# Attention inside a decoder layer: summing the softmax probabilities by GpSimd and accumulating DMAs in place of GpSimd groups, and loops that hint their back edge

## Chip, cores and metric

One core of a Trainium2 chip runs the whole layer in one launch. The metric is device time in microseconds (us); the kernel before takes 5611.14 us, the median of 3 runs (5606.75 to 5614.59).

## What is computed

The layer is self-attention, cross-attention and a gated feed-forward with weights rounded to FP4, each with a residual. Only the self-attention is changed. Its core, per batch element and head (2 x 16 heads of 32 channels, 2048 positions), is run twice, once with a bias that decays with distance and once without:

```python
scores = einsum('bhqd,bhkd->bhqk', q, k) / sqrt(hd)
if bias is not None:
    scores = scores + bias[None, None]
attn = softmax(scores, axis=-1)
out = einsum('bhqk,bhkd->bhqd', attn, v)
...
out = alpha * out_short + (1.0 - alpha) * out_long
```

The softmax needs, per query, the sum of the exponentials over all 2048 keys. The change is about how that sum, the denominator, is formed.

## The kernel before, in words

`project` computes q, k and v in four groups and rounds the feed-forward weights, `attend` does the attention, `finish` the rest. In `attend` a **unit** is one head with one of the two biases: 64 units in all, four to a pass, 16 passes (`UNITS`, `PASSES`). The first and the last pass are written out, and the 14 between them are a loop on each engine (`Fori`), so each engine comes to a back edge 13 times. A unit is 16 **steps** (`KB`), one for each block of 128 keys.

In a step TensorE (PE in the profile) does four things, in an order written out by hand in its `one_pass`:

- `times_v` (L903): four fp32 products of the block's exponentials with v, shown as eight matmuls, into the bank `outputs_T`;
- `scores_for_exp` (L836, tile scores_kq): four pieces of 512 queries of the next blocks' transposed scores, which ScalarE (ACT) exponentiates into `probs_T` (L745), a ring of `PBUF` = 8 blocks of 128 x 2048 fp32;
- `scores_for_max` (L836, tile scores_qk): four pieces of the scores of a later unit, which VectorE (DVE) reduces to row maxima (L764);
- in some steps `count` (L913): the matmuls of a summed group with a matrix of ones, which adds the column sums into the bank `sums`.

The denominator goes by six **groups** of key blocks (`GROUPS`: four of three blocks, two of two). GpSimd (POOL) adds the blocks of a group in SBUF (L704, ten additions of 128 x 2048 a unit) into one of two buffers `group_sum`, and three steps later (`COUNT_LAG`) TensorE counts the group. So there are six counts a unit. After the last one, ScalarE copies the sums out of PSUM (`take_sums`, L724, at its step 4 of the next unit), VectorE inverts them in four pieces (L786, steps 3 to 6, `INVERT`), scales the output (L792, step 8, `WEIGH`) and for every second unit adds the two heads' parts (L799, step 10, `MIX`).

What holds the engines together: GpSimd's queue runs in order, and each addition waits for ScalarE's exponentials of its block and, at the start of a group, for the count that frees the buffer. ScalarE may write block b + 8 only when `times_v` and the addition of block b are done. SyncE's queue loads q, k and v of the unit four further on (L619, L621, L625) when the unit's last transposed scores are done. Nothing in the kernel before is issued as a DMA from GpSimd's queue, and none of its DMAs accumulates.

Of the kernel before, what the change touches and what calls it, by code (L numbers as in the profile page):

```python
# [16 lines left out]
F32 = mybir.dt.float32  # L17
# [190 lines left out]
def project(nc, x, w, weights, xg, x_in, qk_scr, v_scr, w_gate, w_up, w_down, wgu, wd_scr):  # L208
# [4 lines left out]
    with ExitStack() as ctx:  # L213
# [63 lines left out]
        def over_groups(eng, group):  # L277


            with eng.Fori(0, B * NG // 2 - 1) as m:  # L280
# [235 lines left out]
INVERT = 3  # L516
WEIGH = 8
MIX = 10


GROUPS = ((0, 1, 2), (3, 4, 5), (6, 7, 8), (9, 10, 11), (12, 13), (14, 15))
COUNT_LAG = 3
GROUPS_N = len(GROUPS)
ADDS = KB - GROUPS_N


def adds_until(kb):

    return sum(max(0, sum(b <= max(kb, g[1]) for b in g) - 1) for g in GROUPS if g[0] <= kb)

# [11 lines left out]
def attend(nc, qk_scr, v_scr, gates, kinkA, kinkB, pos_scr, attn_scr):  # L542
# [4 lines left out]
    with ExitStack() as ctx:  # L547
# [10 lines left out]
        group_sum = sb("probs_group_sum", [P, 2, L], F32)  # L558
# [32 lines left out]
        counted = Rises(sem("a_counted"), UNITS * GROUPS_N, credit=1)  # L591
# [16 lines left out]
        def _(sp):  # L608
# [64 lines left out]
            with sp.Fori(1, PASSES - 1) as n:  # L673
                one_pass(n, False, False)
# [6 lines left out]
        def _(pool):  # L681
            give_credit(pool, [maxed, expd, summed, added, counted, taken, sums_out, weighed] + stored)
# [7 lines left out]

            def one_pass(n):
                for w in range(UNITS):
                    for g, blocks in enumerate(GROUPS):

                        wait_apart(pool, counted, counted.at(n, w * GROUPS_N + g - 1), passed)
                        total = group_sum[:, g % 2, :]
                        for b in blocks[1:]:

                            wait_apart(pool, expd, expd.at(n, (w * KB + b + 1) * NQ), passed)
                            first = probs[:, blocks[0] % PBUF, :]  # L700
                            if b > blocks[1]:
                                first = total
                                wait_apart(pool, added, added.at(n, w * ADDS + adds_until(b) - 1), passed)
                            nc.gpsimd.tensor_tensor(total, first, probs[:, b % PBUF, :], ALU.add).then_inc(added.sem, 1)  # L704

            with pool.Fori(0, PASSES) as n:
# [3 lines left out]
        def _(act):  # L710
# [10 lines left out]
            def take_sums(w, n):  # L721
                act.wait_ge(counted.sem, counted.at(n, (w + 1) * GROUPS_N))
# [5 lines left out]
            def one_pass(n, first, last):  # L728
                for w in range(UNITS):
                    back = unit_before(w, n, first)  # L730
                    for kb in range(KB):

                        if back and kb == COUNT_LAG + 1:
# [15 lines left out]
            with act.Fori(1, PASSES - 1) as n:  # L749
# [5 lines left out]
        def _(dve):  # L755
# [65 lines left out]
            with dve.Fori(1, PASSES - 1) as n:  # L821
# [9 lines left out]
        def _(pe):  # L831
# [16 lines left out]
            def scores_for_max(w, n, c):  # L848
# [6 lines left out]
                pe.wait_ge(maxed.sem, maxed.at(n, k - 2 + (k - 3) // CHUNKS if k >= 3 else 0))  # L855
# [51 lines left out]
            def count(w, n, g):  # L907

                if g == 0:
                    pe.wait_ge(sums_out.sem, sums_out.at(n, w))  # L910
                pe.wait_ge(added.sem, added.at(n, w * ADDS + adds_until(GROUPS[g][-1])))
                for qt in range(NQ):
                    last = nc.tensor.matmul(pc[qt * HD:(qt + 1) * HD, :], ones[:, :], group_sum[:, g % 2, qt * BANK:(qt + 1) * BANK],  # L913
                                            start=g == 0, stop=g == GROUPS_N - 1)
                last.then_inc(counted.sem, 1)
# [10 lines left out]
            def one_pass(n, first, last):  # L926
                for w in range(UNITS):
# [8 lines left out]
                    for i in range(KB):  # L936
# [8 lines left out]
                        due = [(u, g) for g in range(len(GROUPS)) for u, d in (((w, n), 0), (back, KB))  # L945
# [446 lines left out]
```

## Time and profile before

| | |
|---|---|
| median of 3 runs | 5611.14 us (5606.75 to 5614.59) |
| span of the profiled execution | 5613.5 us (the profile gives no other time for it) |
| TensorE busy | 5382.8 us, 96% of the span |
| VectorE busy | 4180.9 us, 74% |
| ScalarE busy | 2874.8 us, 51% |
| GpSimd busy | 2933.2 us, 52% |
| attention | about 690 to 4280 us of the span |
| mean granted TensorE clock | 0.981 of 2.4 GHz |

Matmuls are pipelined and their recorded ends are modelled, so a TensorE that is busy all the time isn't at its peak. What a stretch costs is read from the distance between the starts of its instructions. "<-issue" means that the engine waited for nothing the profile shows. A DMA's "us to landing" runs from its issue until its semaphore rises.

### The profile page before, as it was taken

The numbers are of one execution on the slowest core, as the hardware profiler recorded it, in microseconds if no ns is written. First come the engines' busy times: TensorE is split into PE (matmuls) and PEld (weight loads), VectorE is DVE, ScalarE is ACT, GpSimd is POOL, SyncE is SP. The second block draws the span as 40 slices with busy tenths as digits, with TensorE's granted clock in tenths as the row PEclk, the third lists the DMA queues.
The fourth block names the chain that finished last, engine by engine and source line by source line (L and its number), as shares of the span: only waits on it lengthen the run. The fifth ranks groups of instructions, "written<-read, shape, count | busy, mean of one in ns | idle before, by whom it ended". The sixth has DMA issues, their size and how long they took to land. (4 is left out here: it accounts for less than half of the span.)

```text
span 5613.5 us, 97704 instructions
## 1 busy us (share of the span) xinstructions
PE 5382.8 (96%) x28780; PEld 2121.9 (38%) x28780; DVE 4180.9 (74%) x7218; ACT 2874.8 (51%) x5201; POOL 2933.2 (52%) x658
## 2 busy tenths in 40 slices
PE   7999899999999999999999999999996999999999
PEld 3444333333322323223233332232332555555555
DVE  5444688877877878778778787787883777777777
ACT  1111166666666666666666666666664333333332
POOL 0000088878877878778778787788884000000000
PEclk9999799999999999999999999999998999999999
DMA  4333201010101010101010101010101000000000
GB/s 135 105 104 93 81 19 33 21 29 22 33 21 29 21 34 21 29 21 33 22 29 21 34 21 29 21 33 22 29 3 49 17 22 17 22 17 22 17 22 12
DMA packets 145632, 191.62 MB, mean 34 GB/s; under 512 B 18500, under 2 KB 97988, under 8 KB 145030
## 3 DMA queue, kind: packets, MB, share of 16 engines
q1 hardware_dynamic: 145159, 185.65, 11.2%
q8 instruction: 255, 4.18, 0.3%
q14 instruction: 218, 1.79, 0.1%
HBM read 123.56 MB, written 61.64 MB: 33 GB/s over the span
## 5 line engine op out<-in xcount | busy, mean ns | idle before, releaser
L764 DVE TENSOR_REDUCE rowmax_parts<-scores_qk 128x1 f32<-128x512 f32 x4096 | 2569.8, 682 | 668.9 <-PE scores_qk L836 666.3
L745 ACT ACTIVATE probs_T<-scores_kq 128x512 f32<-128x512 f32 x4096 | 2263.3, 596 | 1249.5 <-PE scores_kq L836 1195.2
L704 POOL TENSOR_TENSOR probs_group_sum<-probs_T 128x2048 f32<-128x2048 f32 x384 | 1742.4, 4538 | 667.4 <-PE sums L913 395.7
L836 PE MATMUL scores_kq<-q_operand,k_operand 103*128 103x512 f16 (+3 forms) x3712 | 1279.8, 351 | 16.7 <-ACT probs_T L745 15.4
L704 POOL TENSOR_TENSOR probs_group_sum<-probs_group_sum,probs_T 128x2048 f32<-128x2048 f32 x256 | 1185.5, 4631 | 46.0 <-POOL probs_group_sum L704 45.1
L836 PE MATMUL scores_qk<-k_operand,q_operand 96*128 96x512 f16 (+4 forms) x3712 | 1178.9, 354 | 22.8 <-DMA k_operand<-positions_dram 18.5
L903 PE MATMUL outputs_T<-probs_T,v_operand 128*32 128x512 f32 x8192 | 1103.3, 611 | 52.4 <-issue 52.4
L836 PEld LDWEIGHTS scores_qk<-k_operand,q_operand 96*128 96x128 f16 (+1 forms) x3712 | 352.7, 98 | 898.6 <-DVE rowmax_parts L764 627.1
L1341 PE MATMUL f_gate_up<-w_gate_up,xq_T 128*128 128x352 f32 x2048 | 626.4, 462 | 0.8 <-issue 0.8
L836 PEld LDWEIGHTS scores_kq<-q_operand,k_operand 103*128 103x128 f16 x3712 | 361.2, 98 | 672.9 <-ACT probs_T L745 507.1
L1341 PEld LDWEIGHTS f_gate_up<-w_gate_up,xq_T 128*128 128x128 f32 x2048 | 382.5, 190 | 200.7 <-issue 2.6
L913 PE MATMUL sums<-probs_group_sum,ones 128*32 128x512 f32 x3072 | 417.6, 616 | 3.3 <-POOL probs_group_sum L704 3.3
L836 PE MATMUL scores_kq<-q_operand_above,k_operand 103*128 103x512 f16 (+3 forms) x1152 | 398.8, 347 | 0.8 <-ACT probs_T L745 0.6
L836 PE MATMUL scores_qk<-k_operand,q_operand_above 102*128 102x512 f16 (+3 forms) x1152 | 388.0, 352 | 3.8
L473 PE MATMUL products_p<-xn_T,w_qkv 128*128 128x512 f32 x768 | 337.7, 595 | 0.8 <-ACT xn_T L418 0.8
L1330 PE MATMUL f_gate_up<-w_down,hidden_T 128*128 128x512 f32 x704 | 330.8, 597 | 3.4 <-DVE hidden L1249 2.7
L683 POOL MEMSET ones<- 128x32 f32 x1 | 0.1, 124 | 602.5 <-POOLq L213 602.5
L903 PEld LDWEIGHTS outputs_T<-probs_T,v_operand 128*32 128x32 f32 x8192 | 161.8, 108 | 372.2 <-issue 352.0
L786 DVE RECIPROCAL sums_inverse<-sums_T 128x128 f32<-128x128 f32 x256 | 240.7, 942 | 15.5 <-ACT sums_T L724 15.5
L494 PE MATMUL products_p<-w_qkv,xn_T 128*128 128x512 f32 x512 | 221.1, 592 | 0.0
L473 PEld LDWEIGHTS products_p<-xn_T,w_qkv 128*128 128x128 f32 x768 | 144.4, 191 | 172.2 <-issue 172.2
L1128 ACT ACT_TABLE_LOAD x160 | 205.3, 1283 | 2.8
(144 smaller groups left out, 3477.2 us busy)
## 6 DMA issues: line engine op xcount, KB each, us to landing
qk_parts_dram<-qk_parts SPq DMA_DIRECT2D x96, 256.0 KB, 2.5
q_operand<-qk_parts_dram SPq DMA_DIRECT2D x192, 128.0 KB, 2.6
k_operand<-qk_parts_dram SPq DMA_DIRECT2D x192, 128.0 KB, 2.9
v_dram<-v_heads SPq DMA_DIRECT2D x16, 1024.0 KB, 5.4
v_operand<-v_dram SPq DMA_DIRECT2D x64, 256.0 KB, 3.1
q_operand_above<-qk_parts_dram SPq DMA_DIRECT2D x96, 128.0 KB, 2.8
x_groups<-x SPq DMA_DIRECT2D x8, 1024.0 KB, 8.8
attention_dram<-o_mixed SPq DMA_DIRECT2D x128, 64.0 KB, 1.6
```

Source lines behind the costliest of these rows:

```text
L473: last = nc.tensor.matmul(mm[:, m % 4, :], w[:, c, m * P:(m + 1) * P], xT[:, u, c, :], start=c == 0, stop=c == KT - 1)
L494: last = nc.tensor.matmul(mm[:, j % 4, :], xT[:, u, c, t * P:(t + 1) * P], w[:, c, (3 + a) * H:(4 + a) * H], start=c == 0, stop=c == KT - 1)
L704: nc.gpsimd.tensor_tensor(total, first, probs[:, b % PBUF, :], ALU.add).then_inc(added.sem, 1)
L745: nc.scalar.activation(probs[:, kb % PBUF, qt * BANK:(qt + 1) * BANK], pb[:, k % 2, :], ACT.Exp)\
L764: nc.vector.reduce_max(rowmax[:, w % 2, c // NQ, c % NQ:c % NQ + 1], pa[:, k % 3, :], AX.X)\
L786: nc.vector.reciprocal(inv[:, r * P:(r + 1) * P], sums[:, r * P:(r + 1) * P]).then_inc(inverted.sem, 1)
L836: return nc.tensor.matmul(out, lhsT, rhs, start=start, stop=stop, skip_group_check=True)
L903: last = nc.tensor.matmul(po[qt * HD:(qt + 1) * HD, :], v_op[:, w, kb, :], probs[:, kb % PBUF, qt * BANK:(qt + 1) * BANK], start=kb == 0, ...
L913: last = nc.tensor.matmul(pc[qt * HD:(qt + 1) * HD, :], ones[:, :], group_sum[:, g % 2, qt * BANK:(qt + 1) * BANK], start=g == 0, stop=g = ...
L1128: nc.scalar.activation(warmed[:, place:place + 1], eps[:, 0:1], function)
L1330: last = nc.tensor.matmul(pg[:, 0, 0, :], hT[:, c, :], wd[:, c, :], start=c == 0, stop=c == FT - 1)
L1341: last = nc.tensor.matmul(pg[:, k % 2, g, 0:FW], xqT[:, t, c, :], wgu[:, c, g, k * FW:(k + 1) * FW], start=c == 0, stop=c == KT - 1)
```

## The change

- GpSimd now adds nine blocks (0, 1, 3, 5, ... 15) by eight additions into one of two `added_sum` buffers. The other seven (2, 4, ... 14) go by DMAs issued from GpSimd's queue into one buffer, `poured_sum`: the first is a plain copy of 1 MB within SBUF, and the six that follow accumulate. Each waits in GpSimd's queue until the one before it has landed. The first also waits until TensorE has counted the buffer's last content.
- TensorE counts twice a unit: the poured sum in step 3 of the next unit, the added sum in step 4. The order of scores and maxima, which differed in steps with a count, is the same in all steps now.
- ScalarE waits, before it overwrites a block of the ring, for the addition or for the DMA that reads it. It takes the sums at its step 6. VectorE inverts them in steps 6 to 9, weighs at 11 and mixes at 12.
- The waits of TensorE for VectorE at the first three pieces of a pass are written by the piece that used the bank last.
- All loops (in `project`, `attend`, `finish`) carry `hint_back_edge=True`.

The core of the diff:

```diff
-GROUPS = ((0, 1, 2), (3, 4, 5), (6, 7, 8), (9, 10, 11), (12, 13), (14, 15))
-COUNT_LAG = 3
+INVERT = 6
+WEIGH = 11
+MIX = 12
+SUMMED_BY_POOL = (0, 1, 3, 5, 7, 9, 11, 13, 15)
+SUMMED_BY_DMA = (2, 4, 6, 8, 10, 12, 14)
+COUNT_POURED, COUNT_ADDED = 3, 4
+TAKE_SUMS = 6
...
+            def add(w, n, b):
+                total = added_sum[:, w % 2, :]
+                if b == 1:
+                    first = probs[:, 0, :]
+                    wait_apart(pool, counted, counted.at(n, w - 1), passed)
+                else:
+                    first = total
+                    wait_apart(pool, added, added.at(n, w * ADDS + adds_until(b) - 1), passed)
+                wait_apart(pool, expd, expd.at(n, (w * KB + b + 1) * NQ), passed)
+                nc.gpsimd.tensor_tensor(total, first, probs[:, b % PBUF, :], ALU.add).then_inc(added.sem, 1)
+
+            def pour(w, n, b):
+                i = SUMMED_BY_DMA.index(b)
+                wait_apart(pool, expd, expd.at(n, (w * KB + b + 1) * NQ), passed)
+                if i == 0:
+                    wait_apart(pool, counted_poured, counted_poured.at(n, w), passed)
+                    nc.gpsimd.dma_start(poured_sum[:, :], probs[:, b % PBUF, :]).then_inc(poured.sem, 16)
+                else:
+                    wait_apart(pool, poured, poured.at(n, w * POURS + i), passed)
+                    nc.gpsimd.dma_start(poured_sum[:, :], probs[:, b % PBUF, :], accum_op=ALU.add).then_inc(poured.sem, 16)
+
+                    for b in range(1, KB):
+                        if b in SUMMED_BY_DMA:
+                            pour(w, n, b)
+                        else:
+                            add(w, n, b)
...
-                        old = w * KB + kb - PBUF
-                        act.wait_ge(summed.sem, summed.at(n, old + 1))
-                        act.wait_ge(added.sem, added.at(n, old // KB * ADDS + adds_until(old % KB)))
+                        u, b = divmod(w * KB + kb - PBUF, KB)
+                        act.wait_ge(summed.sem, summed.at(n, u * KB + b + 1))
+                        if b not in SUMMED_BY_DMA:
+                            act.wait_ge(added.sem, added.at(n, u * ADDS + adds_until(b)))
+                        elif u >= 0 or not first:
+                            act.wait_ge(poured.sem, poured.at(n, u * POURS + SUMMED_BY_DMA.index(b) + 1))
...
                         times_v(w, n, i)
-                        if due:
-                            maxima(0)
-                            scores(i + 1, 2)
-                            maxima(1)
-                            scores(i + 1, 3)
-                        else:
-                            scores(i + 1, 2)
-                            maxima(0)
-                            scores(i + 1, 3)
-                            maxima(1)
-                        for u, g in due:
-                            count(*u, g)
+                        if back and i == COUNT_POURED:
+                            count_poured(*back)
+                        if back and i == COUNT_ADDED:
+                            count_added(*back)
+                        scores(i + 1, 2)
+                        maxima(0)
+                        scores(i + 1, 3)
+                        maxima(1)
...
-            with pe.Fori(1, PASSES - 1) as n:
+            with nc.Fori(1, PASSES - 1, engines=[pe.engine], hint_back_edge=True) as n:
```

## Rows read from the trace of the kernel before

**Rows 1.** The page: busy time, share of the span and instructions by engine.

```profile
PE 5382.8 (96%) x28780; PEld 2121.9 (38%) x28780; DVE 4180.9 (74%) x7218; ACT 2874.8 (51%) x5201; POOL 2933.2 (52%) x658
```

**Rows 2.** The waits in the attention, 692.9 to 4267.4 us: total, times, longest.

```profile
ACT probs_T L745 <- PE scores_kq L836: 1194.0, 1388, 6.9
...
POOL probs_group_sum L704 <- PE sums L913: 395.7, 126, 10.7
...
PE outputs_T L903 <- issue: 52.4, 13, 4.6
```

**Rows 3.** The timeline of TensorE: plain steps, and the first one with a count.

```profile
2000.13 1.06 PE L903 MATMUL outputs_T<-probs_T,v_operand 128*32 128x512 f32 x8
...
2003.06 1.06 PE L903 MATMUL outputs_T<-probs_T,v_operand 128*32 128x512 f32 x8
...
2004.72 0.38 PE L836 MATMUL scores_kq<-q_operand,k_operand 103*128 103x512 f16 x1
2005.03 1.07 PE L913 MATMUL sums<-probs_group_sum,ones 128*32 128x512 f32 x8
2006.03 0.39 PE L836 MATMUL scores_qk<-k_operand,q_operand 102*128 102x512 f16 x1
2006.25 0.38 PE L836 MATMUL scores_kq<-q_operand,k_operand 103*128 103x512 f16 x1
...
2007.06 1.06 PE L903 MATMUL outputs_T<-probs_T,v_operand 128*32 128x512 f32 x8
```

**Rows 4.** The timeline of TensorE: first product of successive units in one pass.

```profile
2035.04 1.93 PE L903 MATMUL outputs_T<-probs_T,v_operand 128*32 128x512 f32 x8 [3.97 <-issue]
...
2093.08 1.06 PE L903 MATMUL outputs_T<-probs_T,v_operand 128*32 128x512 f32 x8
...
2146.99 1.06 PE L903 MATMUL outputs_T<-probs_T,v_operand 128*32 128x512 f32 x8
...
2201.90 1.06 PE L903 MATMUL outputs_T<-probs_T,v_operand 128*32 128x512 f32 x8
...
2260.51 1.93 PE L903 MATMUL outputs_T<-probs_T,v_operand 128*32 128x512 f32 x8 [3.58 <-issue]
```

**Rows 5.** Stretches at a back edge: length, busy of five engines, granted clock, DMA share, GB/s.

```profile
2031.07:2034.90 3.83, 0.00 (x0) 0.00 (x0) 1.04 (x2) 0.68 (x2) 0.00 (x0) 0.95 0.05 10
2035.00:2041.00 6.00, 5.68 (x20) 0.80 (x20) 1.38 (x2) 1.20 (x2) 0.00 (x0) 0.50 0.02 5
2041.00:2047.00 6.00, 6.00 (x43) 2.03 (x39) 4.15 (x7) 3.41 (x7) 5.35 (x2) 0.97 0.00 0
```

**Rows 6.** The timeline: TensorE's first and last unit, and what ends the attention.

```profile
692.86 1.93 PE L903 MATMUL outputs_T<-probs_T,v_operand 128*32 128x512 f32 x8
...
4223.13 1.06 PE L903 MATMUL outputs_T<-probs_T,v_operand 128*32 128x512 f32 x8
...
4273.35 0.59 ACT L724 COPY sums_T<-sums 128x512 f32<-128x512 f32 x1 [6.43 <-PE sums L913]
```

**Rows 7.** The timeline of VectorE: reciprocals between the maxima.

```profile
2053.31 0.94 DVE L786 RECIPROCAL sums_inverse<-sums_T 128x128 f32<-128x128 f32 x1
2054.17 2.42 DVE L764 TENSOR_REDUCE rowmax_parts<-scores_qk 128x1 f32<-128x512 f32 x4
2056.50 0.94 DVE L786 RECIPROCAL sums_inverse<-sums_T 128x128 f32<-128x128 f32 x1
```

**Rows 8.** The timeline of GpSimd: two additions behind each other.

```profile
2041.48 4.54 POOL L704 TENSOR_TENSOR probs_group_sum<-probs_T 128x2048 f32<-128x2048 f32 x1 [10.61 <-PE sums L913]
2046.20 4.54 POOL L704 TENSOR_TENSOR probs_group_sum<-probs_group_sum,probs_T 128x2048 f32<-128x2048 f32 x1 [0.18 <-POOL probs_group_sum L704]
```

**Rows 9.** DMA issues by tile: KB each, median us from issue to landing.

```profile
v_dram<-v_heads SPq DMA_DIRECT2D x16, 1024.0 KB, 5.4
...
x_groups<-x SPq DMA_DIRECT2D x8, 1024.0 KB, 8.8
...
attention_dram<-o_mixed SPq DMA_DIRECT2D x128, 64.0 KB, 1.6
```

**Rows 10.** Stretches (share and GB/s last): all DMA engines busy, loads, attention; SyncE's issues.

```profile
4290.00:4300.00 10.00, 6.56 (x16) 3.15 (x16) 2.03 (x6) 2.93 (x5) 0.00 (x0) 0.62 1.00 378
...
2024.00:2034.00 10.00, 6.16 (x41) 2.01 (x39) 5.90 (x10) 4.33 (x8) 4.80 (x2) 1.00 0.38 111
...
692.90:4267.40 3574.50, 3497.72 (x22439) 1092.63 (x22442) 2840.61 (x4490) 2298.76 (x4216) 2923.01 (x639) 0.99 0.09 25
...
2025.02 1.26 SPq L619 DMA_DIRECT2D q_operand<-qk_parts_dram  x3
```

**Rows 11.** The chain that ended last, in `finish`: successive tiles, start and length.

```profile
4374.10 4.87 PE f_gate_up L1341 x16
...
4414.45 4.79 PE f_gate_up L1341 x16
...
4454.64 4.87 PE f_gate_up L1341 x16
...
4494.90 4.77 PE f_gate_up L1341 x16
```

**Rows 12.** VectorE's groups over two passes, 2035.0 to 2485.8 us.

```profile
L792 DVE SCALAR_TENSOR_TENSOR o_weighed<-o_T,gates,sums_inverse 128x512 f32<-128x512 f32 x8 | 6.2, 773 | 0.0
...
L799 DVE TENSOR_TENSOR o_mixed<-o_weighed 128x512 f32<-128x512 f32 x4 | 2.7, 684 | 0.0
```

More of the change, by code:

```diff
@@ L277, in over_groups @@
         def over_groups(eng, group):
-            with eng.Fori(0, B * NG // 2 - 1) as m:
+            with nc.Fori(0, B * NG // 2 - 1, engines=[eng.engine], hint_back_edge=True) as m:
                 for u in range(2):
@@ L672, in _ @@
             one_pass(0, True, False)
-            with sp.Fori(1, PASSES - 1) as n:
+            with nc.Fori(1, PASSES - 1, engines=[sp.engine], hint_back_edge=True) as n:
                 one_pass(n, False, False)
@@ L706, in _ @@
-            with pool.Fori(0, PASSES) as n:
+                    for b in range(1, KB):
[3 more added lines that the diff above has]
+                            add(w, n, b)
+            with nc.Fori(0, PASSES, engines=[pool.engine], hint_back_edge=True) as n:
                 one_pass(n)
@@ L748, in _ @@
             one_pass(0, True, False)
-            with act.Fori(1, PASSES - 1) as n:
+            with nc.Fori(1, PASSES - 1, engines=[act.engine], hint_back_edge=True) as n:
                 one_pass(n, False, False)
@@ L820, in _ @@
             one_pass(0, True, False)
-            with dve.Fori(1, PASSES - 1) as n:
+            with nc.Fori(1, PASSES - 1, engines=[dve.engine], hint_back_edge=True) as n:
                 one_pass(n, False, False)
@@ L853, in scores_for_max @@
                     pe.wait_ge(opened[w].sem, opened[w].at(n, opened[w].per_pass))
-                pe.wait_ge(maxed.sem, maxed.at(n, k - 2 + (k - 3) // CHUNKS if k >= 3 else 0))
+                if k >= 3:
+                    pe.wait_ge(maxed.sem, maxed.at(n, k - 2 + (k - 3) // CHUNKS))
+                else:
+                    m = max(j for j in range(UNITS * CHUNKS) if j % 3 == k)
+                    pe.wait_ge(maxed.sem, maxed.before(n, m + 1 + m // CHUNKS))
                 bank = pa[:, k % 3, :]
@@ L971, in _ @@
             end = (UNITS - 1, PASSES - 1)
-            for g in range(GROUPS_N):
-                if GROUPS[g][-1] + COUNT_LAG >= KB:
-                    count(*end, g)
+            count_poured(*end)
+            count_added(*end)
 CTX, CD = 77, 1024
@@ L1067, in over_tiles @@
             step(-1, 1, (1, 2))
-            with eng.Fori(0, NT // 2 - 1) as m:
+            with nc.Fori(0, NT // 2 - 1, engines=[eng.engine], hint_back_edge=True) as m:
                 for t in range(2):
@@ L1094, in _ @@
             sp.dma_start(wd[:, :, :], wd_scr[:, :, :]).then_inc(wd_in, 16)
-            with sp.Fori(0, NT // 2 - 1) as m:
+            with nc.Fori(0, NT // 2 - 1, engines=[sp.engine], hint_back_edge=True) as m:
                 for t in range(2):
```

52 lines of the change are left out of this document (22 added, 30 removed).

## The prediction

> **What bounds the kernel now.** I read the page first. TensorE is busy for 96% of the span, and the change lies in the attention, where VectorE and GpSimd follow at 74% and 52% over all [rows 1]. The waits of that stretch come next: ScalarE waits 1194 us for TensorE's scores, GpSimd 396 us for counts, while TensorE's own matmuls wait only in 13 places, 52.4 us, for nothing the profile shows [rows 2]. So TensorE sets the pace. Its timeline gives the price of its work by the distance of starts: a plain step takes 2.93 us and the step with a count 4.00 [rows 3]. Within that one, the count moves the next score from the usual 0.22 us behind the last to 1.31, so a count costs 1.09 us.
>
> The starts of four successive units [rows 4] are 58.04, 53.91, 54.91 and 58.61 us apart. The two in the middle are plain, with a mean of 54.41; the others hold a back edge. A whole pass is 225.47 us, which is 7.8 more than four plain units. Where it goes is seen in the windows: TensorE does nothing for some 3.9 us, then works for 6 us at a granted clock of 0.50 (1.2 GHz) before it is back at 0.97 [rows 5]. The stall thus costs about 4 us itself and nearly as much again by the clock that follows it. There are 13 of them: 13 x 7.8 = 101 us. As a check, 63 x 54.41 + 101 = 3529, against 3530.3 from the first unit to the last [rows 6].
>
> **The change, part by part.** The sum is made against the profiled execution, span 5613.5 us, which is 2.4 us above the median.
>
> *Counts.* Four of six go: 4 x 1.09 = 4.4 us a unit. All of it is on TensorE, so a unit would fall from 54.4 to 50.0.
>
> *The other engines' schedule.* A step with a reciprocal keeps VectorE busy for 3.19 us (distance of two reciprocals) [rows 7] against TensorE's 2.93 to 3.05. Before, one of the four such steps had a count of TensorE beside it, worth a microsecond of slack. Now steps 6 to 9 have none, at 0.15 to 0.25 us each: +0.8 a unit. The weighing and mixing move between steps of the same kind, ScalarE's copy of the sums likewise; I cost these, the reordering and the waits at a pass's first pieces at nothing, since ScalarE waits for TensorE anyway [rows 2]. If that cover went, each would cost at most its own 0.6 to 0.8 us. TensorE and VectorE together would allow a unit of **50.8 us**.
>
> *GpSimd's queue.* It becomes add, pour, add, pour. An addition takes 4.72 us from start to start [rows 8]. A pour holds the queue while it is issued, and the next one holds it until the last has landed, with the additions behind it. No row shows an issue by GpSimd. SyncE's takes 0.42 us (three in 1.26) [rows 10]; I take 1.0, an estimate, with 0.4 and 2 as bounds.
>
> No row shows an accumulating DMA either. One pass over 1 MB with all 16 engines busy ran at 378 GB/s [rows 10], so 1,048,576 bytes take 2.77 us. What a small DMA needs beside its bytes is about 1.4 us (64 KB landed in 1.6) [rows 9]. If the second read (of the old sum) is hidden behind the first, a pour lands in 1.4 + 2.8 = 4.2 us. If it is not, in 1.4 + 5.5 = 6.9. If it also runs at the rate of the store of 1 MB (5.4 us, so 4.0 beside the 1.4), in 1.4 + 8.0 = 9.4. I take 6.9, since a pour must fetch two operands for each it writes, and its rows of 8 KB are long like those of the 378 GB/s stretch and not short like the store's.
> The Trainium skill (Collectives: The Full Stack, The bandwidth ceiling) says the same of reductions in general: two reads for each write, half of a copy's rate. No run here shows it yet. Its page DMA: Bandwidth & Descriptors (Anatomy of one DMA) gives about 2.0 us plus bytes over 436 GB/s for a DMA issued from GpSimd. With two reads that is 6.8 us, with one 4.4, and the sum below would be 51.6 or, with the queue no longer deciding, 50.8.
>
> The unit on GpSimd's queue: the first pour is plain and lands behind the addition, 1.0 + 4.72 = 5.7. Five more go by the landing, 5 x 6.9 = 34.5. The seventh is followed by two additions (15, then 1 of the next unit), which cover it: 1.0 + 2 x 4.72 = 10.4. That is 50.6. SyncE's loads of the later unit are on the same 16 DMA engines and fall on pour 12: a share of 0.38 over 10 us is 3.8 us of all engines [rows 10]. Half of it is taken: +1.9, bounds 0 and 3.8. So the queue needs **52.5 us** a unit, and it, not TensorE, sets the pace by 1.7 us. TensorE's count of the poured sum then waits for the last pour, and ScalarE's ring of eight blocks takes up the lag until then.
>
> *Back edges.* With the stall and the half clock gone, the 101 us go. The queue must not hide them: 52.5 a unit holds for every unit. In `finish` tiles are 40.35, 40.19 and 40.26 us apart, with or without a back edge [rows 11], so at most 0.1 us for each of 14: nothing. `project` has two back edges and no wait for them.
>
> *The end.* The last unit had 50.2 us from its first product to the copy of its sums [rows 6]. Now its seven pours follow each other from about 10.7 us on: 10.7 + 5.7 + 5 x 6.9 + 6.9 = 57.8, and two counts make it 60: +10.
>
> **Sum:** 63 x 52.5 = 3307.5 for 3530.3, which is -222.8, +10: -213. From 5613.5 that is 5400.5, and against the median **5398 us**.
>
> **Rivals.**
> - *The pours keep up.* If most of the second read is hidden or the loads don't collide, TensorE and VectorE set 50.8 us: 63 x 50.8 = 3200, -330 and nothing at the end: **5281**. For it: the DMA engines' share in the attention is only 0.09 [rows 10]. Against it: two operands pass through each engine for each result. Chance 0.20.
> - *Slower: the chain of pours is the bound.* Each microsecond of landing costs five a unit. The queue needs 18.0 + 5 x landing, so it passes the mean unit of before (3530.3 / 63 = 56.0) at a landing of 7.6 us, only 0.7 above my value. At 9.4 a unit is 65.0: 63 x 9.0 = +567, and the end's +25: **6203**. TensorE would then idle several microseconds a unit, and it has been seen what a stall of 4 us does to its clock [rows 5]. For it: a plain DMA of 1 MB already took 5.4 us as a store and 8.8 as x's load, in shorter rows and beside others [rows 9]. Against it: long rows ran at 378 GB/s. Chance 0.21.
> - *VectorE holds GpSimd off.* The weighing and half a mixing a unit, 0.77 + 0.34 = 1.1 us [rows 12], read two operands from SBUF. If GpSimd's issues have to wait for all of that, a unit takes 53.6: 63 x 1.1 = +69, **5467**. For it speaks only that both touch SBUF; against it, additions follow each other by 4.72 us beside VectorE's work [rows 8]. Chance 0.04.
>   [...]
> - *The hint does nothing.* TensorE's stall (7.8 a pass) is then mostly taken up by the queue's margin (4 x 1.7), but GpSimd's own fetch would stand in its chain: 13 x 4 = 52 us more, **5450**. Against it: the stalls come once a pass, at the back edge and nowhere else [rows 2, 4]. Chance 0.08.
> - *It comes out even*, the landing at 7.6: 0.03.
>
> **How the numbers follow.** The forecast's own case (landing 6.4 to 7.4, 5300 to 5560) has 0.44. The range must take in the 5281 and leave out the upper part of the slow case: 5260 to 5690, which is a landing up to 7.8 us. Some 0.16 lie above and 0.03 below. A measurement of this kernel tells about 0.2% (11 us) from no change. Faster: 0.44 + 0.20 + 0.04 + 0.08 = 0.76; same 0.03; slower 0.21.
>
> **What would show it.** The median landing of `poured_sum` 6.4 to 7.4 us, the DMA share in the attention near (2.8 + 6 x 5.5) / 52.5 + 0.09 = 0.77. GpSimd idle before every other pour, not for ScalarE but for its own DMA. Two counts a unit, steps of 3.0 us without one, about 3.2 in steps 6 to 9. No wait "<-issue" of 4 us and no stretch at clock 0.50 every pass. It is wrong if the landing is over 7.6 (then GpSimd's wait grows in every pair and ScalarE waits for `poured_sum`), or if TensorE waits nowhere in a unit (then the pours keep up).

## The result: 195 us slower, and the profile after

The changed kernel takes **5806.65 us** (median of 4 runs, 5802.63 to 5819.8) against 5611.6 us of the kernel before on the same chip: a ratio of 1.0352, 95% interval 1.0338 to 1.0367. The forecast was 5398 us with a range of 5260 to 5690, so it had both the sign and the range wrong.

The page of the kernel after, its lines on engines, clock, DMA share, the two DMA queues and the groups that matter (line 706 is an addition, 717 an accumulating pour, 938 a count, 931 the product with v):

```profile
span 5800.3 us, 95123 instructions
...
PE 5238.4 (90%) x26732; PEld 2122.1 (37%) x26732; DVE 4268.2 (74%) x7218; ACT 2901.8 (50%) x5201; POOL 2707.7 (47%) x978
...
PEclk9999799999999999999999999999998999999999
DMA  4332376666666666667666676666665000000000
...
q0 software_dynamic: 64512, 469.79, 37.9%
q1 hardware_dynamic: 145159, 185.65, 10.8%
...
L717 POOL DMA_DIRECT2D probs_poured<-probs_T x384 | 338.9, 883 | 932.3 <-DMA probs_poured<-probs_T 697.8
...
L938 PE MATMUL sums<-probs_poured,ones 128*32 128x512 f32 x512 | 87.6, 762 | 132.5 <-DMA probs_poured<-probs_T 132.4
...
probs_poured<-probs_T POOLq DMA_DIRECT2D x448, 1024.0 KB, 7.2
```

TensorE is busy for 144 us less than before [rows 1], in a span that is 187 us longer. So it no longer sets the pace throughout: 90% against 96%. The mean granted clock fell from 0.981 to 0.956 of 2.4 GHz. The counts did go (4 x 1.09 us in 63 units are 275 us), and more than that came back, as idle time and as matmuls at half clock.

The waits in the attention show where (700 to 4400 us; total, times, longest), to be held against [rows 2]:

```profile
ACT probs_T L769 <- PE scores_kq L860: 1341.9, 1322, 9.4
...
POOL probs_poured L717 <- DMA probs_poured<-probs_T: 689.3, 231, 5.8
...
PEld sums L938 <- DMA probs_poured<-probs_T: 136.5, 43, 5.2
PE sums L938 <- DMA probs_poured<-probs_T: 116.0, 47, 4.7
...
PE scores_qk L860 <- DVE rowmax_parts L788: 128.2, 112, 3.9
...
POOL probs_poured L714 <- PE sums L938: 109.7, 43, 6.3
...
PE outputs_T L931 <- issue: 86.9, 13, 7.5
...
PE scores_kq L860 <- DMA q_operand_above<-negmax_T: 28.2, 25, 2.5
```

Before, TensorE's matmuls had one large wait, the 13 at back edges (and 15.2 us in 25 short waits for ScalarE, which the forecast passed over). Now there are four: for the last pour at the count (47 times), for VectorE's maxima (112 times), for SyncE's load of a unit's negated row maxima, `negmax_T`, in its step 14 (25 times), and still the 13 at the back edges, with 86.9 us in place of 52.4.

**What a unit costs, step by step.** From first product to first product a step's length can be read, and its mean taken over the 13 passes from the second to the 14th. The table sets the kernel after beside an experiment described below, plain_psum. There TensorE has no wait for a pour in a pass and none for `negmax_T`, and its waits for the maxima are down to 28.2 us (us; four units of a pass):

| unit | step 3, after / there | steps 11 to 14, after / there | step 15, after / there | unit, after / there |
|---|---|---|---|---|
| 0 | 4.25 / 3.91 | 19.04 / 13.07 | 3.02 / 3.02 | 60.36 / 54.00 |
| 1 | 7.48 / 3.79 | 14.43 / 11.89 | 3.41 / 3.02 | 56.66 / 50.03 |
| 2 | 6.59 / 3.91 | 16.02 / 13.10 | 3.02 / 3.02 | 57.29 / 51.65 |
| 3 | 8.24 / 3.79 | 12.98 / 11.90 | 9.77 / 7.88 | 62.42 / 54.89 |

Over all 63 distances the mean unit is 58.66 us against 56.04 before: 63 x 2.62 = +165 us. The end adds 16, and about 5 lie outside the attention, which makes the 187. Against plain_psum's 52.30, the differences of the columns sum to 11.2, 12.5 and 2.3 us a pass. Scaled to 63 units that is **176 us at the count of the pours, 197 us in steps 11 to 14, where the weighing and mixing lie**, and 36 us in step 15. Not all of the 197 us is VectorE's. In units 1 and 3, which have no mixing, step 14 alone is longer by 2.5 us a pass, 40 us over all. There TensorE waits for the load of `negmax_T`. That is a DMA of 4 KB, which landed in 1.7 us before and in 5.5 us in the kernel after (medians), and psum_operands (experiment 4), which has no delay on VectorE, still waits 24.9 us for it. So these 40 us are put down to the pours' traffic; no run isolates them.

**The first place, GpSimd's queue** (timeline; start, length, then in brackets the idle time before and what ended it). The forecast had these gaps at 6.9 us:

```profile
2001.30 0.88 POOL L717 DMA_DIRECT2D probs_poured<-probs_T  x1 [3.70 <-ACT probs_T L769]
2001.91 4.84 POOL L706 TENSOR_TENSOR probs_added<-probs_added,probs_T 128x2048 f32<-128x2048 f32 x1
2008.83 0.88 POOL L717 DMA_DIRECT2D probs_poured<-probs_T  x1 [2.08 <-DMA probs_poured<-probs_T]
2009.44 4.84 POOL L706 TENSOR_TENSOR probs_added<-probs_added,probs_T 128x2048 f32<-128x2048 f32 x1
2016.38 0.88 POOL L717 DMA_DIRECT2D probs_poured<-probs_T  x1 [2.09 <-DMA probs_poured<-probs_T]
...
2023.93 0.88 POOL L717 DMA_DIRECT2D probs_poured<-probs_T  x1 [2.11 <-DMA probs_poured<-probs_T]
...
2033.13 0.88 POOL L717 DMA_DIRECT2D probs_poured<-probs_T  x1 [3.76 <-DMA probs_poured<-probs_T]
2033.74 4.83 POOL L706 TENSOR_TENSOR probs_added<-probs_added,probs_T 128x2048 f32<-128x2048 f32 x1
2038.23 4.79 POOL L706 TENSOR_TENSOR probs_added<-probs_T 128x2048 f32<-128x2048 f32 x1
2046.38 0.59 POOL L714 DMA_DIRECT2D probs_poured<-probs_T  x1 [3.35 <-PE sums L938]
```

Successive pours start 7.53, 7.55, 7.55 and 9.20 us apart: each time the landing of the last one ends the wait. The addition lies inside the gap and is no bound (a pour's row is 0.88 us long, but the addition starts 0.61 behind it). From a landing to the start of the pour that waited for it pass 0.57 us, nearly always. The last line shows the chain start anew: the first pour of a unit waits until TensorE has counted the buffer.

TensorE at that count, in its timeline and in windows (columns as in [rows 5]; the last window is the whole attention):

```profile
2038.41 1.06 PE L931 MATMUL outputs_T<-probs_T,v_operand 128*32 128x512 f32 x8
...
2043.81 1.94 PE L938 MATMUL sums<-probs_poured,ones 128*32 128x512 f32 x8 [4.33 <-DMA probs_poured<-probs_T]
```

```profile
2038.41:2043.80 5.39, 1.06 (x9) 0.15 (x8) 1.19 (x2) 0.73 (x2) 4.62 (x2) 0.90 0.58 141
2043.80:2049.00 5.20, 5.19 (x18) 1.45 (x18) 1.99 (x4) 1.63 (x3) 2.60 (x2) 0.50 0.30 112
2049.00:2055.00 6.00, 6.00 (x39) 1.85 (x39) 3.35 (x6) 3.72 (x8) 5.44 (x3) 0.96 0.63 167
692.90:4400.00 3707.10, 3322.20 (x20245) 1086.26 (x20245) 2921.14 (x4486) 2300.12 (x4169) 2662.90 (x946) 0.95 0.67 149
```

It idles 4.33 us for the pour and then works 5.2 us at a granted clock of 0.50, as after a back edge before. A late pour is paid nearly twice, and since the next chain starts behind that count, GpSimd's queue gets the delay as well.

**The second place, VectorE** (timeline of one stretch, GpSimd, VectorE and TensorE together; 816 weighs, 823 mixes, 788 is a row maximum):

```profile
2129.82 4.84 POOL L706 TENSOR_TENSOR probs_added<-probs_added,probs_T 128x2048 f32<-128x2048 f32 x1
...
2131.92 3.30 DVE L816 SCALAR_TENSOR_TENSOR o_weighed<-o_T,gates,sums_inverse 128x512 f32<-128x512 f32 x1
...
2135.88 0.39 PE L860 MATMUL scores_qk<-k_operand,q_operand 96*128 96x512 f16 x1 [2.48 <-DVE rowmax_parts L788]
...
2138.85 4.84 POOL L706 TENSOR_TENSOR probs_added<-probs_added,probs_T 128x2048 f32<-128x2048 f32 x1
...
2140.52 3.73 DVE L823 TENSOR_TENSOR o_mixed<-o_weighed 128x512 f32<-128x512 f32 x1
```

A weighing that took 0.77 us [rows 12] takes 3.30: it begins 2.1 us into an addition of GpSimd and ends at 2135.22, 0.56 us after the addition's end (2134.66). TensorE's next score then waits for the maximum that was queued behind it. The tiles' own lines (least, median, longest in ns) show it for all of them; before they were 739/774/4552 and 680/682/692:

```profile
L816 DVE SCALAR_TENSOR_TENSOR o_weighed<-o_T,gates,sums_inverse x64: 742/1640/4678, 786.0 to 4459.5; 128x512 f32<-128x512 f32 x64
L823 DVE TENSOR_TENSOR o_mixed<-o_weighed x32: 682/2540/4556, 848.5 to 4460.3; 128x512 f32<-128x512 f32 x32
```

The Trainium skill (SBUF — State Buffer, SBUF: two separate sides) states just this: a VectorE operation with two SBUF inputs and a GpSimd operation that reads SBUF hold one pair of ports exclusively, whichever starts first, and the other is blocked until it ends. The trace agrees: the weighing above ends 0.56 us after the addition that it ran into.

### The profile page after: what moved, and what is told of

Same layout as the page of the kernel before. It is cut to its first block and busy times, and to the rows that moved or that the text cites. A ratio compares the mean times of both kernels' runs of the same rounds, so it can differ in the third digit from the quotient of the medians.

```text
span 5800.3 us, 95123 instructions
## 1 busy us (share of the span) xinstructions
PE 5238.4 (90%) x26732; PEld 2122.1 (37%) x26732; DVE 4268.2 (74%) x7218; ACT 2901.8 (50%) x5201; POOL 2707.7 (47%) x978
## 3 DMA queue, kind: packets, MB, share of 16 engines
q0 software_dynamic: 64512, 469.79, 37.9%
## 5 line engine op out<-in xcount | busy, mean ns | idle before, releaser
L788 DVE TENSOR_REDUCE rowmax_parts<-scores_qk 128x1 f32<-128x512 f32 x4096 | 2534.3, 679 | 750.0 <-PE scores_qk L860 749.6
L769 ACT ACTIVATE probs_T<-scores_kq 128x512 f32<-128x512 f32 x4096 | 2298.4, 597 | 1418.4 <-PE scores_kq L860 1357.3
L706 POOL TENSOR_TENSOR probs_added<-probs_added,probs_T 128x2048 f32<-128x2048 f32 x448 | 2145.9, 4790 | 9.8 <-ACT probs_T L769 9.0
L860 PE MATMUL scores_kq<-q_operand,k_operand 103*128 103x512 f16 (+3 forms) x3712 | 1310.0, 358 | 42.2 <-DMA q_operand_above<-negmax_T 28.6
L860 PE MATMUL scores_qk<-k_operand,q_operand 96*128 96x512 f16 (+4 forms) x3712 | 1150.3, 360 | 108.4 <-DVE rowmax_parts L788 77.9
L931 PE MATMUL outputs_T<-probs_T,v_operand 128*32 128x512 f32 x8192 | 1127.6, 623 | 87.8 <-issue 86.9
L717 POOL DMA_DIRECT2D probs_poured<-probs_T x384 | 338.9, 883 | 932.3 <-DMA probs_poured<-probs_T 697.8
L706 POOL TENSOR_TENSOR probs_added<-probs_T 128x2048 f32<-128x2048 f32 x64 | 308.0, 4812 | 64.9 <-ACT probs_T L769 64.9
L860 PEld LDWEIGHTS scores_kq<-q_operand_above,k_operand 103*128 103x128 f16 x1152 | 113.0, 98 | 350.4 <-ACT probs_T L769 293.8
L938 PE MATMUL sums<-probs_poured,ones 128*32 128x512 f32 x512 | 87.6, 762 | 132.5 <-DMA probs_poured<-probs_T 132.4
```

The costliest lines, as they stand in the source:

```text
L717: nc.gpsimd.dma_start(poured_sum[:, :], probs[:, b % PBUF, :], accum_op=ALU.add).then_inc(poured.sem, 16)
L769: nc.scalar.activation(probs[:, kb % PBUF, qt * BANK:(qt + 1) * BANK], pb[:, k % 2, :], ACT.Exp)\
L788: nc.vector.reduce_max(rowmax[:, w % 2, c // NQ, c % NQ:c % NQ + 1], pa[:, k % 3, :], AX.X)\
L860: return nc.tensor.matmul(out, lhsT, rhs, start=start, stop=stop, skip_group_check=True)
L931: last = nc.tensor.matmul(po[qt * HD:(qt + 1) * HD, :], v_op[:, w, kb, :], probs[:, kb % PBUF, qt * BANK:(qt + 1) * BANK], start=kb == 0, ...
L938: mm = nc.tensor.matmul(pc[qt * HD:(qt + 1) * HD, :], ones[:, :], src[:, qt * BANK:(qt + 1) * BANK], start=first, stop=last)
```

## The experiments

Each ran beside the kernel before on its own chip, where that one took 5612 to 5613 us. Each quotation is the text on record before the run.

**1 and 2. The hint alone, in both kernels.** hints_only is the kernel before with the hint on all loops, no_hints the kernel after without it.

```diff
-            with pe.Fori(1, PASSES - 1) as n:
+            with nc.Fori(1, PASSES - 1, engines=[pe.engine], hint_back_edge=True) as n:
```

> The kernel before with nothing changed but the hint on every loop's back edge. If the hint removes the fetch and the half clock behind it, the 13 stalls of 4 us and the clock go: about 5510 us. If the hint does nothing for a body of this size, the 13 stalls stay at 3.6 to 4.6 us and the time stays at 5611 within 10 us. The changed kernel's 13 stalls (6.7 us each) speak for the second.

> The changed kernel without the hints. If the hint does nothing: 5807 us within 12. If it does save part of the fetch, slower by up to 50 us, and the 13 stalls longer than 6.7 us.

hints_only: 5574.23 us, ratio 0.9929 (0.9912 to 0.9945). no_hints: 5857.77, ratio 1.0432 (1.0415 to 1.045). The hint is worth 38 us in the kernel before and 51 in the kernel after, neither the whole 101 nor nothing, so neither branch of the first expectation came true. The trace of hints_only shows what is left at a back edge (TensorE's waits, one of its products, and the window behind it):

```profile
PE outputs_T L903 <- issue: 16.5, 9, 2.2
```

```profile
1128.78 1.75 PE L903 MATMUL outputs_T<-probs_T,v_operand 128*32 128x512 f32 x8 [1.72 <-issue]
```

```profile
1129.00:1135.00 6.00, 5.87 (x32) 1.19 (x28) 2.42 (x4) 1.89 (x4) 1.01 (x1) 0.72 0.02 5
```

The stall falls from 4.0 us to about 1.8, and a lower clock still follows it, now a mean of 0.72 over 6 us. In the kernel after the stall is longer: 86.9 us / 13 = 6.7 with the hint, and 101.8 / 13 = 7.8 without.

**3. Pours that don't accumulate.** plain_pours copies each poured block over the last one, so that six of the seven are missing from the denominator; ScalarE's copy adds 1.0 so that it isn't zero.

```diff
-                    nc.gpsimd.dma_start(poured_sum[:, :], probs[:, b % PBUF, :], accum_op=ALU.add).then_inc(poured.sem, 16)
+                    nc.gpsimd.dma_start(poured_sum[:, :], probs[:, b % PBUF, :]).then_inc(poured.sem, 16)
```

> The changed kernel with the six accumulating DMAs of a unit turned into plain copies of the same 1 MB. Left out: six of seven poured blocks from the denominators (a constant 1 is added to the sums so that none is zero). Theory 1, the chain of pours is the bound: landing falls from 7.2 to about 4.4 us, the chain to some 45 us a unit, TensorE no longer waits for it, and the time falls to about 5500 to 5600. Theory 2, TensorE's own stalls (blocked VectorE, back edges, half clock) are the bound: it stays above 5700.

5789.46 us, ratio 1.0315 (1.0297 to 1.0332). The landing fell from 7.2 to 4.6 us, the pours' share of the DMA engines from 37.9% to 21.2%, and TensorE's wait at the count went: step 3 is 3.8 to 3.9 us in every unit. Yet only 17 us were gained. The page's line and those of the two tiles tell why:

```profile
probs_poured<-probs_T POOLq DMA_DIRECT2D x448, 1024.0 KB, 4.6
```

```profile
L816 DVE SCALAR_TENSOR_TENSOR o_weighed<-o_T,gates,sums_inverse x64: 751/3718/3973, 777.7 to 4445.0; 128x512 f32<-128x512 f32 x64
L823 DVE TENSOR_TENSOR o_mixed<-o_weighed x32: 681/3685/4887, 843.4 to 4445.8; 128x512 f32<-128x512 f32 x32
```

With the pours out of the way, weighing and mixing start early in an addition nearly every time: the median is 3.7 us each. Steps 11 to 14 are 6.5 us a unit longer than in plain_psum (26.0 a pass), where they were 3.1 in the kernel after. No matmul waits for `negmax_T` here. What one place gave up, the other took. It came out as the second expectation (above 5700) had it.

**4. Weighing and mixing with one operand in PSUM.** psum_operands writes the inverse sums, and the odd unit's weighed output, into a PSUM bank that is free then, and mixes right behind the weighing. All is computed. It puts a few waits of VectorE and TensorE for that bank in.

```diff
-                nc.vector.reciprocal(inv[:, r * P:(r + 1) * P], sums[:, r * P:(r + 1) * P]).then_inc(inverted.sem, 1)
+                nc.vector.reciprocal(pt[:, r * P:(r + 1) * P], sums[:, r * P:(r + 1) * P]).then_inc(inverted.sem, 1)
...
-                nc.vector.tensor_tensor(o_mix[:, p, :], o_w[:, 0, :], o_w[:, 1, :], ALU.add).then_inc(mixed.sem, 1)
+                nc.vector.tensor_tensor(o_mix[:, p, :], o_w[:, 0, :], pt[:, :], ALU.add).then_inc(mixed.sem, 1)
```

> The changed kernel with the inverse sums, and the second weighed output, kept in PSUM (bank turned), so that VectorE's weighing and mixing have one SBUF operand each, the mixing follows the weighing in step 11, and TensorE's transpose waits for both. If two SBUF operands make VectorE wait for GpSimd's addition, the weighing falls from a mean of 1.96 to about 0.8 us and the mixing from 2.65 to 0.8. If TensorE's side set the pace everywhere that would be 2.2 us a unit, 140 in all. If the chain of pours is the bound in most units, under 60 us come back, most of it in the units that follow a back edge.

5831.52 us, ratio 1.0388 (1.0371 to 1.0405): 25 us slower than the kernel after, where the expectation had up to 140 us or under 60 us come back, though the cause of delay on VectorE is gone. The weighing (now with `turned` in PSUM) is short every time; TensorE's wait for the pours has doubled:

```profile
L816 DVE SCALAR_TENSOR_TENSOR o_weighed<-o_T,gates,turned x32: 734/736/747, 781.5 to 4438.5; 128x512 f32<-128x512 f32 x32
```

```profile
PEld sums L938 <- DMA probs_poured<-probs_T: 276.1, 43, 9.6
PE sums L938 <- DMA probs_poured<-probs_T: 252.7, 47, 8.7
```

The time moved to step 3: 13.84, 8.85 and 11.72 us in units 1, 2 and 3. So with the lock gone the chain of pours alone makes the kernel as slow as the changed one, and (experiment 3) the lock alone does too.

**5. Both at once.** plain_psum is 3 and 4 together. If two bounds of nearly equal height stand behind each other, only this one falls far.

> Both edits at once: plain copies in place of the accumulating DMAs, and VectorE's second operand in PSUM. Left out, as before: six of seven poured blocks from the denominators (1 is added to the sums). Apart they gave 5789 and 5832 us. Theory A, two bounds of nearly the same height (the chain of pours by its landing, VectorE held by GpSimd's additions), each of which stays when only the other is taken away: together they leave TensorE's own 50.7 us a unit and some 2 for the back edge, so 5440 us, within 40. Theory B, something else sets 58.7 us a unit (GpSimd's additions, the half clock, the reordered steps): it stays above 5700.

**5391.49 us**, ratio 0.9609 (0.9593 to 0.9625). It is 49 us below the 5440 of theory A, 9 more than its margin. Alone the two edits gave -17 and +25 us, together -415. That settles the cause: two bounds, each of which alone holds the unit near 58.7 us (58.69 in experiment 3, 59.00 in experiment 4), and below them 52.30. Its units without a back edge are 50.04 and 51.65 us, mean 50.85; the forecast for TensorE and VectorE together was 50.8.

**6. Two buffers for the pours.** two_psum is 4 with `poured_sum` doubled, a semaphore for each, and counts, copy and inversions one step later. The chain no longer waits for TensorE's count.

```diff
-        poured_sum = sb("probs_poured", [P, L], F32)
+        poured_sum = sb("probs_poured", [P, 2, L], F32)
...
-                    wait_apart(pool, counted_poured, counted_poured.at(n, w), passed)
+                    wait_apart(pool, counted_poured, counted_poured.at(n, w - 1), passed)
```

> Accumulating pours as in the changed kernel, but into two buffers that alternate by unit (with a semaphore each), so that the first pour of a unit doesn't wait for TensorE's count; counts a step later, VectorE's operand in PSUM. If the coupling of the chain's start to TensorE's step 3 is what costs, the unit falls to TensorE's 53: 5450 us. If the chain's own length does (gaps of 5.2 + 42.0 + 9.6 in the changed kernel's trace), it stays at 56 to 57 a unit: 5700 us, within 50.

5751.68 us, ratio 1.0241 (1.0224 to 1.0258): 80 us less than experiment 4, but still slower than before, at the upper end of the second branch (5700, within 50). The 80 us are what the second buffer and the later count give together; how much of it is the coupling of TensorE's and the queue's delays, no run separates. What is left is the chain's own length: the mean unit is 57.95 us (56 to 57 expected), and GpSimd still waits 902 us for its own DMAs.

**7 and 9. Five pours in place of seven**, GpSimd adding eleven blocks, with the operands in PSUM (five_psum) and in SBUF as they were (five_only). The diff is what both have; five_psum has the edit of experiment 4 besides.

```diff
-SUMMED_BY_POOL = (0, 1, 3, 5, 7, 9, 11, 13, 15)
-SUMMED_BY_DMA = (2, 4, 6, 8, 10, 12, 14)
+SUMMED_BY_POOL = (0, 1, 2, 4, 5, 7, 8, 10, 11, 13, 14)
+SUMMED_BY_DMA = (3, 6, 9, 12, 15)
```

> Five blocks (3, 6, 9, 12, 15) poured, eleven added by ten additions, two additions between any two pours, VectorE's operand in PSUM. All is computed. The landing of 7.2 us lies behind two additions of 4.75, so nothing waits for it; GpSimd's queue needs 10 x 4.75 + 5 x 0.6 = 50.5 us a unit, TensorE about 52.8. Theory A gives 5440 us, within 50. If GpSimd's additions are slowed further by DMAs, or TensorE waits for the last pour, 5500 to 5600.

> The changed kernel with five blocks poured and eleven added, and nothing else: VectorE's weighing and mixing read two SBUF operands again. All is computed. Beside the run with five pours and the operand in PSUM (5491 us) it prices VectorE's wait for GpSimd's additions where the chain of pours is no bound. If that wait is as in the plain copies (some 6.4 us a unit between the two runs with and without it), about 5750 to 5850 us. If it was only a partner of the chain, 5491 to 5560.

five_psum: **5490.73 us**, ratio 0.9782 (0.9765 to 0.9798), with all computed and pours that land in 7.6 us. A pour is now due every third step, 8.8 us or more, and keeps up: no pour waits for the one before it. The time lies 51 us above the 5440 expected, for TensorE still waits 34.8 us for last pours, and the back edges cost more (below). five_only: 5670.73, ratio 1.0097 (1.0079 to 1.0116). That is between its two branches: the wait costs 2.9 us a unit here, not 6.4. The 180 us between the two runs are the edit of experiment 4, which moves the operand to PSUM and the mixing from step 12 to step 11. What moving the mixing alone would give was not run. The mixing shows it most plainly: in step 12 it starts some 0.4 us into an addition (2098.65 against 2098.28 in one case) and waits it out, 5 us in the median.

```profile
L816 DVE SCALAR_TENSOR_TENSOR o_weighed<-o_T,gates,sums_inverse x64: 750/1639/2855, 782.5 to 4326.8; 128x512 f32<-128x512 f32 x64
L823 DVE TENSOR_TENSOR o_mixed<-o_weighed x32: 691/4965/5004, 840.5 to 4327.6; 128x512 f32<-128x512 f32 x32
```

In five_psum each back edge costs more, for TensorE stalls twice (its timeline behind one of them):

```profile
1112.28 1.93 PE L931 MATMUL outputs_T<-probs_T,v_operand 128*32 128x512 f32 x8 [4.18 <-issue]
...
1118.60 0.61 PE L860 MATMUL scores_kq<-q_operand,k_operand 103*128 103x512 f16 x1 [3.42 <-issue]
```

**8. Shorter loads.** short_loads cuts SyncE's loads of q and k to 128 of 2048 columns after the first pass (most of q and k is then stale), to see what the chain loses to other traffic.

```diff
+                cols = L if isinstance(n, int) and n == 0 else BANK // 4
-                    sp.dma_start(k_op[w][r * HD:(r + 1) * HD, :], scr(1 + a, part)).then_inc(s, 16)
+                    sp.dma_start(k_op[w][r * HD:(r + 1) * HD, 0:cols], scr(1 + a, part)[:, 0:cols]).then_inc(s, 16)
```

> The changed kernel with SyncE's loads of q and k cut to their first 128 of 2048 columns from the second pass on, the same number of DMAs. Left out: the rest of q and k, so the heads of the first pass are used again there. If the loads lengthen the chain, the gap from pour 12 to pour 14 falls from a mean of 9.4 to about 7.6 us and the stall at the back edge from 6.7 to near 4, and 1 to 3 us a unit come back: 5620 to 5740. If they don't, within 20 us of 5807.

5737.41 us (two runs, 5724.04 and 5750.78), ratio 1.0223 (1.0192 to 1.0253): 69 us less than the kernel after, 1.1 a unit, at the upper end of what was expected. The median landing stays at 7.2. The gap from pour 12 to pour 14 fell from 9.4 to 8.4 us, not to 7.6, and the stall at the back edge from 6.7 to 6.4, not to 4. The loads feel the pours too: v's landed in 7.8 us in the kernel after, against 3.1 without pours (hints_only).

**10 and 11. Fewer back edges.** The 14 passes of the loop become two iterations of seven on TensorE, VectorE, ScalarE and SyncE: one back edge in place of 13. GpSimd's loop is left as it is; it runs over all 16 passes, so it has 15 back edges and not the 13 given above for each engine. five_psum_unrolled does it to experiment 7, before_unrolled to the kernel before, without any hint.

```diff
-            with pe.Fori(1, PASSES - 1) as n:
-                one_pass(n, False, False)
+            with pe.Fori(0, (PASSES - 2) // 7) as m:
+                for j in range(7):
+                    one_pass(m * 7 + j + 1, False, False)
```

> Five pours, operand in PSUM, and the loop over 14 passes in the attention written as two iterations of seven passes each, so 1 back edge in place of 13. All is computed. A back edge cost the run with five pours about 4.3 us in step 15 and 6.7 in steps 0 and 1, 11 in all: 12 x 11 = 132, so 5360 us, within 25. If fetching straight code stalls too beside the pours' traffic, 5400 to 5490.

> The kernel before with the same two iterations of seven passes and no hint. A back edge costs 7.8 us there by its trace (stall and half clock), so 12 x 7.8 = 94 less: 5518 us, within 12. If the stall comes from the size of the code and not from the branch, 5611.

five_psum_unrolled: **5367.36 us**, ratio 0.956 (0.9544 to 0.9576), the best of all, with everything computed. before_unrolled: 5518.96, ratio 0.983 (0.9813 to 0.9846), 94 us less than before; 12 x 7.8 = 94 was the price that the profile of before gave. The first one's waits and group lines:

```profile
PE outputs_T L934 <- issue: 4.6, 1, 4.6
```

```profile
L706 POOL TENSOR_TENSOR probs_added<-probs_added,probs_T 128x2048 f32<-128x2048 f32 x576 | 2668.2, 4632 | 124.4 <-ACT probs_T L769 70.5
...
L706 POOL TENSOR_TENSOR probs_added<-probs_T 128x2048 f32<-128x2048 f32 x64 | 300.6, 4696 | 81.2 <-ACT probs_T L769 80.4
...
L717 POOL DMA_DIRECT2D probs_poured<-probs_T x256 | 224.1, 876 | 2.4 <-ACT probs_T L769 2.4
```

A pour no longer waits for the one before it. The mean unit is 51.73 us. Little is left on GpSimd: (2668.2 + 300.6) / 64 = 46.4 us of additions a unit and five issues of 0.6 make 49.4. So the idea of the change is worth 152 us on top of unrolling (5518.96 to 5367.36), with five pours, without the lock and with the hint on what loops are left. The Trainium skill (Runtime: NRT & Kernel Launch, Instruction fetch mechanics) says that a taken branch out of the fetched pages stalls the engine, and that kernels are better unrolled for it; the trace agrees, 4.0 us a stall and as much again by the clock.

## Why the prediction was wrong

**Right: TensorE's side.** Four counts went at their price, plain steps are 2.93 to 3.05 us, those with a reciprocal 3.08 to 3.26, and a unit with nothing in its way 50.85 us (forecast 50.8).

**Wrong: "the queue needs 52.5 us a unit".** Term by term, by the mean gaps between the pours' starts in the kernel after (units 5 to 56 of 64):

| term | forecast | measured |
|---|---|---|
| first pour, plain | 5.7 | 5.24 |
| five gaps, with the loads | 5 x 6.9 + 1.9 = 36.4 | 8.42 + 7.58 + 8.65 + 7.93 + 9.45 = 42.03 |
| last pour to the next unit's first | 10.4 | 11.88 |
| unit | 52.5 | 59.15 |

The large miss is in the second row, and it isn't the price of a pour. The two reads were as argued: a plain pour occupies the engines 0.212 x 5786.3 / 448 = 2.74 us (forecast 2.77), an accumulating one (0.379 x 5800.3 - 64 x 2.74) / 384 = 5.27 (forecast 5.54). An accumulating pour that nothing disturbs lands in 6.95 us, the least of 384, against 6.9. Inside it two errors cancel: its bytes take 0.27 less than forecast, and what lies beside them is 1.7 us, not 1.4.

Two things lengthen the gap. The sum had no term for the 0.57 us from a landing to the next pour's start: 5 x 0.57 = 2.9 us a unit. And other traffic adds 42.03 - 5 x (6.95 + 0.57) = 4.4 us where 1.9 was taken, above the bound of 3.8; the five landings take 7.8 us in the mean. The measured sum, 5 x (6.95 + 0.57) + 4.4, is 5.6 us above the forecast's 36.4: 0.3 by the landing itself, 2.8 by the hand-over, 2.5 by the traffic. The third row was out as well. A pour after two additions starts 9.55 us after the last one at the least, under the 10.4 forecast; the rest of the 11.88 is mostly the wait for TensorE's count (43 times, 109.7 us).

The median landing of 7.2 lay inside the 6.4 to 7.4 that the forecast gave itself, and the unit was out all the same. That median is over all 448 pours, 64 plain ones among them; the accumulating ones alone have 7.5. The Trainium skill (DMA: Bandwidth & Descriptors, Anatomy of one DMA) gives a formula by which I had estimated 6.8 with two reads and 4.4 with one; the least measured are 6.95 and 4.4. With 6.8 the forecast's sum would have been 52.0 a unit, not the 51.6 that it states.

**Wrong: "the weighing and mixing move between steps of the same kind; if that cover went, each would cost at most its own 0.6 to 0.8 us".** The steps are of the same kind for TensorE, not for GpSimd. In two passes of before (2000 to 2460 us) there are 13 weighings and mixings, and every one began 4.3 to 4.4 us into an addition, ended 0.55 to 0.62 us after that addition's end, and had the next addition start 0.3 to 0.4 us after its own start. One of them:

```profile
2062.26 4.53 POOL L704 TENSOR_TENSOR probs_group_sum<-probs_T 128x2048 f32<-128x2048 f32 x1 [1.05 <-ACT probs_T L745]
2066.66 0.74 DVE L792 SCALAR_TENSOR_TENSOR o_weighed<-o_T,gates,sums_inverse 128x512 f32<-128x512 f32 x1
2066.97 4.84 POOL L704 TENSOR_TENSOR probs_group_sum<-probs_group_sum,probs_T 128x2048 f32<-128x2048 f32 x1 [0.18 <-POOL probs_group_sum L704]
```

They were tied to the additions then too, but fell just where one ended; the next addition took 4.84 us in place of 4.54. In the same stretch of the kernel after, eleven of the twelve end 0.55 to 0.57 us behind an addition as well, but begin up to 3.2 us before its end; the twelfth meets none and takes 0.74. The cost is the rest of an addition, up to 4.4 us (the mixings of five_only), and not the operation's own time. The rival "VectorE holds GpSimd off" had the right pair and the wrong loser: the short operation is blocked by the long one. The row that spoke against it, additions 4.72 us apart [rows 8], could only show that GpSimd isn't held up.

**Wrong: "with the stall and the half clock gone, the 101 us go".** The hint takes 38 of 101 in the kernel before (experiment 1), and in the kernel after a stall of 6.7 us remains. Unrolling removed 94 us of the 101 in the kernel before (experiment 11).

**Wrong in kind: bounds taken as a maximum.** "ScalarE's ring of eight blocks takes up the lag until then" holds for ScalarE (it waits 0.2 us for the pours in all), but the count waits up to 4.7 us (116.0 us in 47 waits), the clock falls to 0.50 behind the one shown, and the single buffer passes TensorE's delay back to the queue. Experiment 6 gives at most 80 us for the last part. The pours' traffic also reached a DMA that the forecast left out, the 4 KB load of `negmax_T`: some 40 us.

**The end**: 4388.85 to 4455.36 is 66.5 us against 50.2, +16 where I had +10. TensorE's last count waits 16.4 us for the last pour.

**The slower rival** had the mechanism, the place (TensorE idle in each unit, clock down) and a chance of 0.21. Its condition, a landing over 7.6, was not met: by its own 18.0 + 5 x 7.2 a unit would be 54.0 and the kernel faster than before. Even with 7.8, the mean of the accumulating landings, and without the 1.9 for traffic that the 18.0 holds, it would be 16.1 + 5 x 7.8 = 55.1, still under the 56.0 of before. Its outcome came by terms that its formula lacks: the hand-over, more traffic, and VectorE. Of the signs that I had named, GpSimd's wait for its own DMA came (689 us), and the DMA share was 0.67 where 0.77 was forecast: (2.74 + 6 x 5.27) / 58.66 + 0.09 = 0.68, so the missing part is mostly the longer unit. The wait "<-issue" and the half clock, whose absence was forecast, stayed.

**What stays open.** Where the rest of the 4.4 us of extra traffic a unit comes from; short_loads took only q's and k's, and its five gaps are 1.3 us shorter. Why VectorE's delay costs 6.5 us a unit in plain_pours and 2.9 with five pours: an addition begins at another time there, and no run sets that time on purpose. Why TensorE stalls a second time behind a back edge with five pours. The kernel after with its own seven pours was not unrolled.

## What to carry to other kernels

Price a chain of dependent DMAs by the distance of issues (landing, hand-over and the traffic beside it), not by the landing, and give it slack: seven pours a unit, at least 7.5 us apart, did not fit into 51 us; five, with two additions between them, did. Before moving a VectorE operation with two SBUF operands beside work of GpSimd, look at what GpSimd runs in that step. The price here was the rest of its operation, and one operand in PSUM avoided it. When undoing either of two suspects changes nothing, undo both before acquitting them.

## What the runs showed of the hardware that was not expected

- GpSimd's additions take 4.83 us beside accumulating pours (median of the kernel after, 4832 ns) and 4.54 beside plain ones (mean 4533 ns in plain_pours, as before). No run tells why.
- A back edge's stall on TensorE was longer the more the DMA engines were busy. With the hint it took 1.8 us at a DMA share of 0.09 (hints_only), 4.3 at 0.41 (plain_pours), 4.8 at 0.47 (plain_psum) and 6.7 at 0.67 (the kernel after); without it 4.0 at 0.09 and 7.8 at 0.66 (no_hints).
- A 4 KB DMA of SyncE (`negmax_T`) landed in 1.7 us before and in 5.5 in the kernel after (medians); in plain_pours and in five_psum it was 1.7 again.
- From the landing of a pour to the start of the next, which GpSimd's queue held back for it, passed 0.57 us, nearly always.
- A VectorE operation of 0.68 us took 5.0 in the median behind GpSimd's additions (five_only), and 0.69 with an operand in PSUM (five_psum).
